# Recurrent part of a decoder: output product in three passes by block pairs, second norm on ScalarE, weight halves split at other places

## What is computed

```python
x = layernorm(x, ln0_w, ln0_b)
for l in range(4):
    h = layernorm(x, ln1_w[l], ln1_b[l])
    hh = time_shift(h)                       # the token before
    xk, xv, xr = (h * t[l] + hh * (1 - t[l]) for t in (tmk, tmv, tmr))
    k, v, sr = xk @ Wk[l].T, xv @ Wv[l].T, sigmoid(xr @ Wr[l].T)
    x = x + (sr * wkv(time_decay[l], time_first[l], k, v)) @ Wo[l].T
    h = layernorm(x, ln2_w[l], ln2_b[l])
    hh = time_shift(h)
    xk, xr = h * cmk[l] + hh * (1 - cmk[l]), h * cmr[l] + hh * (1 - cmr[l])
    kf = square(relu(xk @ Wck[l].T))         # 1024 hidden units
    x = x + sigmoid(xr @ Wcr[l].T) * (kf @ Wcv[l].T)
```

## Times and profile before

| what | us |
|---|---|
| median of 3 runs | 1903.39 (1900.92 to 1904.49) |
| profiled execution, its own time | 1903.27 |
| its span | 1901.6 |
| PE busy | 1777.8 (93%) |
| DVE busy | 1233.4 (65%) |
| ACT busy | 841.2 (44%) |
| mean granted clock of TensorE | 0.97 of 2.4 GHz |

### The profile page before, as it was taken

One profiled execution on the slowest core, in us unless ns is written; L12 is line 12 of the kernel. 1 busy time (PEld: TensorE's weight loads), 2 busy tenths in 40 slices (PEclk: granted clock), 3 DMA queues, 4 the chain that ended last, 5 costly groups with the idle time before them and its releaser, 6 DMA issues.

```text
span 1901.6 us, 26356 instructions
## 1 busy us (share of the span) xinstructions
PE 1777.8 (93%) x10124; PEld 1527.4 (80%) x10124; DVE 1233.4 (65%) x1953; ACT 841.2 (44%) x1304; POOL 3.6 (0%) x26
## 2 busy tenths in 40 slices
PE   2399999999999988889799999999999999999997
PEld 1277787877787767788789899889998898998896
DVE  6889999989999943788644445445445444454445
ACT  3465676665667634344332333333333323333333
POOL 0000000000000000000000000000000000000000
PEclk9699999999999998899899999999999999999999
DMA  3000001001001002111021111011100001011001
GB/s 111 5 23 17 10 25 40 6 8 43 17 12 50 1 0 88 52 43 37 10 77 34 34 34 34 0 33 33 33 33 0 33 33 33 33 34 38 1 1 39
DMA packets 35274, 56.54 MB, mean 30 GB/s; under 512 B 3094, under 2 KB 20476, under 8 KB 34684
## 3 DMA queue, kind: packets, MB, share of 16 engines
q1 hardware_dynamic: 35196, 55.47, 9.0%
HBM read 51.79 MB, written 3.67 MB: 29 GB/s over the span
## 4 chain that ended last, share of the span: by engine, by line
PE 49%; DVE 1%; ACT 0%; issue 0%; ACTq 0%; DVEq 0%
PE fbanks L1662 16%; PE fbank L1662 16%; PE fbank L1678 16%; DVE acc L1517 0%; DVE fst L1543 0%; PE fbank L52 0%; DVE xk L1541 0%; ACT acc L1633 0%; PE fbanks L1695 0%; ACT acc L1610 0%; DVE fmv L1546 0%; DVE fyy L1557 0%; DVE frstd L1558 0%; DVE fyy L1556 0%; ACTq L1340 0%
## 5 line engine op out<-in xcount | busy, mean ns | idle before, releaser
L1493 DVE TENSOR_TENSOR hf<-sil,fbanks 128x512 f32<-128x512 f32 (+1 forms) x128 | 79.4, 620 | 332.1 <-PE fbanks L1662 273.4
L1601 ACT ACTIVATE sil<-fbanks 128x512 f32<-128x512 f32 (+1 forms) x128 | 69.6, 544 | 442.2 <-PE fbanks L1662 442.2
L1678 PE MATMUL fbank<-wl,hh 128*128 128x256 f32 x896 | 250.3, 279 | 0.0
L1678 PE MATMUL fbank<-wh,hl 128*128 128x256 f32 x896 | 250.1, 279 | 0.0
L1678 PE MATMUL fbank<-wh,hh 128*128 128x256 f32 x896 | 250.1, 279 | 0.0
L1493 DVE TENSOR_TENSOR hf<-sil,fbank 128x512 f32<-128x512 f32 (+1 forms) x128 | 79.5, 621 | 149.8 <-PE fbank L1662 142.8
L715 PE MATMUL pair<-wcv,kf 128*112 128x256 f32 x768 | 176.1, 379 | 0.0
L1678 PEld LDWEIGHTS fbank<-wl,hh 128*128 128x128 f32 x896 | 168.3, 188 | 2.2
L1678 PEld LDWEIGHTS fbank<-wh,hh 128*128 128x128 f32 x896 | 168.4, 188 | 1.8
L1678 PEld LDWEIGHTS fbank<-wh,hl 128*128 128x128 f32 x896 | 168.4, 188 | 0.0
L1500 DVE TENSOR_TENSOR hl<-hf,hh 128x512 fp32r<-128x512 f32 (+1 forms) x256 | 158.3, 618 | 0.0
(11 more groups left out here) (237 smaller groups left out, 3478.3 us busy)
## 6 DMA issues: line engine op xcount, KB each, us to landing
raw<-in_w_gate SPq DMA_DIRECT2D x16, 512.0 KB, 3.8
raw<-in_w_up SPq DMA_DIRECT2D x16, 512.0 KB, 4.7
raw<-in_w_down SPq DMA_DIRECT2D x16, 512.0 KB, 5.6
raw<-in_w_ck SPq DMA_DIRECT2D x4, 1024.0 KB, 4.8
wcv<-in_w_cv SPq DMA_DIRECT2D x4, 768.0 KB, 4.4
raw<-in_ctx_t SPq DMA_DIRECT2D x4, 750.0 KB, 6.4
ct<-in_ctx_t SPq DMA_DIRECT2D x4, 750.0 KB, 5.0
x<-in_x SPq DMA_DIRECT2D x4, 448.0 KB, 6.2
```

Source lines behind the costliest of these rows:

```text
L1493: dve.tensor_tensor(hf[i][:, 0:w], sil[i][:, 0:w], bank[2 * i + 1][:, 0:w], ALU.mult).then_inc(hf_ready, 1)
L1601: act.activation(sil[f % 2][:, 0:w], bank[2 * (f % 2)][:, 0:w], ACT.Silu).then_inc(sil_ready, 1)
L1678: ins = pe.matmul(bank[4 + 2 * (t % 2) + i // 2][:, (i % 2) * C:(i % 2 + 1) * C], a[t % 2][:, f, i * P:(i + 1) * P], m[h][:, DOWN + f * C: ...
```

## The change

- The whole channel output is split in three matmuls. Weights wcvh and wcvl hold all eight blocks, plain wcv and its load are gone, the stage is loaded with all 1 MB of wcv. ACT writes a high part and DVE a low part of all four pairs of the hidden activation. `channel_out` runs over pairs of blocks outside and sequences inside, two pairs before the transposes of norm 1 and two behind them.
- Norm 2 is normalised by ACT, like norm 1, with a shift that DVE writes. ACT's normalise 1 goes ahead of the seed of norm 2.
- The mixes for cr and ck lose their difference: ACT writes h of the token before, scaled by 1 - mu (`past`), and DVE adds h times mu to it.
- DVE's numerator goes ahead of the mixes of norm 1, so ACT's copy of v can come sooner. `diff` shares memory with `dk`, `ckl` with `mix_ck`, `kfl` with `kf`.
- High and low parts of wck are taken just before `high_ck` and just after `low_ck`. The high part of wcv is taken right behind the gate, its low part behind the sums. `low_kf` 1 and 2 lie on either side of the sums, `low_kf` 3 in the next step behind the statistics of norm 2.

```diff
-SPLIT = 2
-NAMES = ["ln1w", "ln1b", "tmk", "tmv", "tmr", "td", "u", "ln2w", "ln2b", "cmk", "cmr", "w"]
+FT = F // P
+NAMES = ["ln1w", "ln1b", "tmk", "tmv", "tmr", "td", "u", "ln2w", "ln2b", "cmk", "cmr", "w", "pmk", "pmr"]
 PRM = {n: i for i, n in enumerate(NAMES)}
-NPRM = len(NAMES)
+NPRM, NPRM_IN = len(NAMES), NAMES.index("w")
...
-        wcvh, wcvl = sb("wcvh", [P, SPLIT * C], F32R), sb("wcvl", [P, SPLIT * C], F32R)
-        wcv = sb("wcv", [P, (F // P - SPLIT) * C])
...
-        ckh, ckl = sb("ckh", [P, CB, G * T], F32R), sb("ckl", [P, CB, G * T], F32R)
-        kf = [sb(f"kf{i}", [P, 2, G * T]) for i in range(4)]
-        kfh, kfl = sb("kfh", [P, SPLIT, G * T], F32R), sb("kfl", [P, SPLIT, G * T], F32R)
+        ckh = sb("ckh", [P, CB, G * T], F32R)
+        with nc.sbuf_tensor("mix_ck", [P, CB, G, T], FP32) as t:
+            mixed["ck"] = t
+        ckl = sb("ckl", [P, CB, G * T], F32R)
+        with nc.sbuf_tensor("kf", [P, FT, G * T], FP32) as t:
+            kf = [t[:, 2 * j:2 * j + 2] for j in range(FT // 2)]
+        t = sb("kfl", [P, FT, G * T], F32R)
+        kfl = [t[:, 2 * j:2 * j + 2] for j in range(FT // 2)]
+        kfh = sb("kfh", [P, FT, G * T], F32R)
...
-                if name == "cv":
-                    w = w[:, 0:SPLIT * C]
...
+            def mix2(m, i, name, mu):
+                for b in range(CB):
+                    dve.wait_ge(past_ready, 2 * CB * m + CB * i + b + 1)
+                    dve.scalar_tensor_tensor(mixed[name][:, b], h[2][:, b, :, 1:T1], param(m, b, mu),
+                                             mixed[name][:, b], ALU.mult, ALU.add).then_inc(mix2_ready, 1)
...
             first_norm(0)
             for s in range(-3, STEPS + 1):
                 if valid(s):
                     after(add_wkv(s))
                     stats(2, chunk(s))
-                    if s % GROUPS == 0:
-                        l = s // GROUPS
-                        low_weights(2 * l, wckl, wckh, ck_done, 4 * GROUPS * l)
+                if valid(s - 1):
+                    low_kf(s - 1, 3)
                 if valid(s + 1):
                     wkv_denominator(s + 1)
                 if valid(s):
                     rsqrt(2, s)
-                    normalise(2, xn[2], chunk(s), xn_ready[2])
+                    set_shift(2)
+                if valid(s + 1):
+                    wkv_numerator(s + 1)
                 if valid(s + 2):
-                    n = difference(1, s + 2)
-                    mix(1, s + 2, ("k", "v", "r"), ("tmk", "tmv", "tmr"), mix1_ready, n)
+                    mix1(s + 2)
                 if valid(s):
-                    n = difference(2, s)
-                    mix(2, s, ("cr",), ("cmr",), mix2_ready, n)
+                    mix2(s, 0, "cr", "cmr")
                 if valid(s - 1):
                     gate_channel(s - 1)
                 if valid(s):
-                    mix(2, s, ("ck",), ("cmk",), mix2_ready, n)
-                if valid(s + 1):
-                    wkv_numerator(s + 1)
+                    mix2(s, 1, "ck", "cmk")
                 if valid(s - 1):
                     add_channel(s - 1)
                 if valid(s):
                     low_ck(s)
+                    if s % GROUPS == 0:
+                        l = s // GROUPS
+                        low_weights(2 * l, wckl, wckh, ck_done, 4 * GROUPS * l)
                 if valid(s + 3):
                     if s + 3 >= GROUPS:
...
                     wkv_out(s + 1)
                 if valid(s + 2):
                     wkv_arguments(s + 2)
-                if valid(s) and s % GROUPS == 0:
-                    l = s // GROUPS
-                    low_weights(2 * l + 1, wcvl, wcvh, cv_done, 2 * GROUPS * l)
                 if valid(s):
                     low_kf(s, 0)
                 if valid(s + 3):
                     rsqrt(1, s + 3)
-                    set_shift(s + 3)
+                    set_shift(1)
                 if valid(s):
-                    for j in range(1, SPLIT // 2):
-                        low_kf(s, j)
+                    low_kf(s, 1)
                 if valid(s + 2):
                     wkv_sums(s + 2)
+                if valid(s):
+                    if s % GROUPS == 0:
+                        l = s // GROUPS
+                        low_weights(2 * l + 1, wcvl, wcvh, cv_done, 2 * GROUPS * l)
+                    low_kf(s, 2)
...
+            def past(m, i, name, mu):
+                act.wait_ge(h_ready[2], CB * (m + 1))
+                if m:
+                    act.wait_ge(*((cr_done, m) if name == "cr" else (ck_done, 4 * m)))
+                for b in range(CB):
+                    act.activation(mixed[name][:, b], h[2][:, b, :, 0:T], ACT.Copy, scale=param(m, b, mu))\
+                        .then_inc(past_ready, 1)
+            def normalise(k, m):
+                act.wait_ge(shift_ready[k], m + 1)
                 xc = x[:, (m % GROUPS) * G:(m % GROUPS + 1) * G, :]
                 for i in range(G):
-                    ins = act.activation(xn[1][:, i, :], xc[:, i, :], ACT.Identity, bias=shift[:, i:i + 1],
-                                         scale=rstd[1][:, i:i + 1])
-                ins.then_inc(xn_ready[1], 1)
+                    ins = act.activation(xn[k][:, i, :], xc[:, i, :], ACT.Identity, bias=shift[k][:, i:i + 1],
+                                         scale=rstd[k][:, i:i + 1])
+                ins.then_inc(xn_ready[k], 1)
...
             def hidden(m, j):
                 act.wait_ge(ck_done, 4 * m + j + 1)
-                split = 2 * j < SPLIT
-                if m and split:
-                    act.wait_ge(kfl_ready, SPLIT // 2 * (m - 1) + j + 1)
-                if m and not split:
+                if m and j == 0:
                     act.wait_ge(cv_done, 2 * m)
                 t = kf[j]
-                act.activation(t[:], pair[HIDDEN[j]][:, :, 0:G * T], ACT.Relu).then_inc(relu_done, 1)
+                act.activation(t, pair[HIDDEN[j]][:, :, 0:G * T], ACT.Relu).then_inc(relu_done, 1)
                 act.wait_ge(relu_done, 4 * m + j + 1)
-                act.activation(t[:], t[:], ACT.Square).then_inc(square_done, 1)
-                if not split:
-                    return
+                act.activation(t, t, ACT.Square).then_inc(square_done, 1)
                 act.wait_ge(square_done, 4 * m + j + 1)
-                if m and j == 0:
-                    act.wait_ge(cv_done, 2 * m)
-                act.activation(kfh[:, 2 * j:2 * j + 2], t[:], ACT.Copy).then_inc(kfh_ready, 1)
+                act.activation(kfh[:, 2 * j:2 * j + 2], t, ACT.Copy).then_inc(kfh_ready, 1)
...
             rsqrt0(0, 0)
             for s in range(-3, STEPS + 1):
-                if valid(s) and s % GROUPS == 0:
-                    l = s // GROUPS
-                    high_weights(2 * l, wckh, ck_done, 4 * GROUPS * l)
                 if valid(s + 1):
                     wkv_exp(s + 1, 2)
+                if valid(s + 2):
+                    normalise(1, s + 2)
                 if valid(s):
                     rsqrt0(2, s)
-                if valid(s + 2):
-                    normalise1(s + 2)
                 if valid(s + 1):
                     reciprocal0(s + 1)
                 if valid(s + 2):
                     norm_out(1, s + 2, pair[2], "ln1w", "ln1b")
                 if valid(s):
+                    normalise(2, s)
                     norm_out(2, s, pair[0], "ln2w", "ln2b")
+                    past(s, 0, "cr", "pmr")
                 if s < 0:
                     rsqrt0(1, s + 3)
                 if valid(s + 2):
                     out(s + 2, 0, kp[:, :, :, 1:T1], k_out)
                 if valid(s):
+                    past(s, 1, "ck", "pmk")
+                    if s % GROUPS == 0:
+                        l = s // GROUPS
+                        high_weights(2 * l, wckh, ck_done, 4 * GROUPS * l)
                     high_ck(s)
                 if valid(s + 2):
                     if s + 2:
...
                     out(s + 2, 2, th[:], th_ready, ACT.Tanh, 0.5)
                 if valid(s):
                     gate(s)
+                    if s % GROUPS == 0:
+                        l = s // GROUPS
+                        high_weights(2 * l + 1, wcvh, cv_done, 2 * GROUPS * l)
                 if valid(s + 2) or valid(s):
                     act.preload_act_table_set(LN_EXP)
                 if s >= 0 and valid(s + 3):
...
                 if valid(s + 2):
                     wkv_exp(s + 2, 0)
                     wkv_exp(s + 2, 1)
-                if valid(s) and s % GROUPS == 0:
-                    l = s // GROUPS
-                    high_weights(2 * l + 1, wcvh, cv_done, 2 * GROUPS * l)
...
+            def channel_out(m, pairs):
+                for p in pairs:
+                    pe.wait_ge(kfl_ready, FT // 2 * m + p + 1)
+                    for i in range(G):
+                        for f in range(2):
+                            j = 2 * p + f
```

(74 more changed lines are left out.)

41 lines of the change are left out of this document (13 added, 28 removed).

## The result

| | before | after |
|---|---|---|
| median us | 1903.94 (1900.92 to 1905.38, 4 runs) | 1927.9 (1926.12 to 1928.33, 4 runs) |
| profiled execution's span | 1901.6 | 1926.6 |
| PE, DVE, ACT busy us | 1777.8, 1233.4, 841.2 | 1760.9, 1252.2, 960.7 |

The ratio is 1.0126, with a 95% interval of 1.0109 to 1.0144: slower by 24 us. The forecast was 1922, its range 1897 to 1936.

What follows compares the result with a forecast made beforehand. PE bound the recurrent part, DVE close; after the change ACT's string would. From 1903.27 us: head to second K +4.9, layer 0's ordinary steps -1.9, later first steps +25.5, other ordinary steps -3.6, tail -6, giving 1922; range 1897 to 1936.

Steps and rivals of the forecast that it cites:

- ordinary step: Recurrent steps not first in a layer: from one k product start (K) to the next 39.95 us, before 40.55.
- ACT's wait for the load: First step of a layer: ACT idles some 2.5 us behind the gate until the load of wcv lands at K + 16.1.
- channel output of the first step from: First step of a layer: PE idles 7.5 us for the low part of wcv, ready at K + 34.5.
- loss to the clock, a first step: First step of a layer: PE's idle lowers the granted clock, costing 2.4 us, bounds 0 to 3.4.
- first step: First step of each layer, K to K: 49.9 us against 41.4, so +8.5.
- head, up to the K of step 0: Start up to step 0's k product: numerator slips into a wait, low wck leaves the path; 4.5 us less.
- tail: Steps 14, 15 and the end: channel output is on the path three times, each 1.9 us or more shorter; 6 less.
- attention and experts: Code behind the recurrent part: untouched by the change, so no change in time.
- Rival A: Recurrent part: PE's saving decides, all 16 steps fall to 38.6 us and the first-step wait is filled; 1872 us; chance 0.07.
- Rival C: Ordinary step: three full engines, new forms at upper bounds or handshakes adding up, 41 instead of 39.95; 1935 us; chance 0.12.
- Rival B: First step: if wcv is loaded before the gate ends, ACT never stands; step near 43, 1895 us; chance 0.11.
- Rival D: First step: only the wait is lost, not the clock, four times 2.4 less; 1912.5 us; 0.68 together with the main case.

Runs made afterwards that it cites:

- e5: Changed kernel plus 56 idle matmuls on PE ahead of the wait for the low part of wcv: 1919.5 us, against 1927.9 for the changed kernel.
- e6: Changed kernel plus two extra ACT copies into an unused tile in steps 0 to 13, ahead of the exponentials: 1946.6 us, ordinary step 40.95.
- e7: Changed kernel plus the same two extra ACT copies, but ahead of the first table load: 1927.7 us, ordinary step 39.88.
- e9: Changed kernel with ACT's eu and normalise 1 ahead of hidden 2 and 3, and DVE's low kf 2 behind the denominator: 1930.9 us.
- e11: Changed kernel with norm 2 normalised on DVE again, all else kept: 1935.9 us, ordinary steps 40.8.
- e10: e3 plus a new order on ACT (normalise 1, affine part, normalise 2 earlier) and DVE (numerator behind norm 1's mixes): 1873.6 us, ratio 0.9840 to the kernel before.
- e1: Changed kernel with a staging tile of its own for wcv, its load issued a layer early: 1918.2 us, ratio 1.0067 to the kernel before.
- e2: Changed kernel with the low part of wcv taken on DVE ahead of the sums, one stage: 1914.7 us, ratio 1.0046 to the kernel before.
- e3: Changed kernel with both own stage for wcv and low part of wcv ahead of the sums: 1900.8 us, ratio 0.9982 to the kernel before.
- e8: Changed kernel with ACT's eu and normalise 1 ahead of hidden 2 and 3, and DVE's low kf 3 behind rsqrt 2: 1940.5 us.

## Why the prediction was right, point by point

| step of the prediction | forecast | measured |
|---|---|---|
| PE's channel output | 11.5 us, 0.118 a matmul | 5.7 for each half, 0.118 |
| ordinary step | 39.95 | 39.87 |
| PE's wait ahead of the transposes | 1.3 | 1.20 |
| ACT's wait for the load | 2.5, high wcv from K + 16.1 | 2.32, K + 16.0 |
| channel output of the first step from | K + 34.5, idle 7.5 | K + 34.7, idle 7.51 |
| loss to the clock, a first step | 2.4 (0 to 3.4) | mean 2.2 by e5 (1.3 to 2.8) |
| first step | 49.9 | 48.8, 49.9, 50.5 |
| head, up to the K of step 0 | -4.5 | -1.7 |
| tail | -6 | -6.1 |
| attention and experts | 0 | +4.3 |

**The ordinary step.** PE's saving was real, 1.9 us, and 0.7 of it arrived. e6 and e7 show why: ACT's string from the gate to normalise 1 sets the step. e9 and e11 show the second path, DVE's to mix_k, right behind it. Rival A falls with that. It is what e10 comes near to, but only with another order on two engines. Rival C did not come: the new forms cost what their nearest rows did, the scaled pair 1.22 or 1.23 against 1.21.

**The first step.** Both waits are where they were put, and e1, e2 and e3 give their price: 10 and 13 us alone, 27 together. Rival B named the right mechanism. Its condition, a load that is done before the gate ends, is what e1 makes, and e3 lands where B's arithmetic pointed (first step near 43, 1895 forecast, 1900.8 measured). What B left out is that the wait for the low part has to go as well. The rule of the Trainium skill that ACT and DVE are strictly first in, first out (TensorE: Matmul & The Clock Gate, "Engine queue depths") agrees again: nothing on ACT passed high wcv in its 2.32 us.

**The clock.** I took 2.4 us from one idle of 4.29 in the tail. e5 puts it at 2.2 in the mean and at 1.3 to 2.8 in single steps, inside my bounds. Rival D, that the clock costs nothing, is refuted.

**What was off.** The head: the numerator did slip into the wait for h, but of the 3.3 us it freed most was lost at once. The exponentials stand behind ACT's tanh of r, which waits for PE, and DVE stood 2.74 us for them, where before it did not wait at all. I had walked DVE through the head, but not ACT. The last link is another too: DVE's difference ahead of mix_k comes 2.6 us earlier than before (94.77 against 97.38), but K only 1.7, right behind the transposes of norm 2, for which PE stood 7.48 us until ACT's normalise 2. DVE and PE of after:

```profile
75.89 2.04 DVE L348 TENSOR_TENSOR_SCAN bb<-e1b,e2b 128x904 f32<-128x904 f32 x1 [2.74 <-ACT e2b L575]
...
96.07 1.76 PE L670 MATMUL pair<-ident,xn 112*128 112x112 f32 x8 [7.48 <-ACT xn L533]
```

The seven traces in which the head has the order of after (after, e1, e2, e3, e5, e6, e7) put the K of step 0 at 96.7 to 99.2 us, so the -1.7 of one execution is uncertain by more than 1 us, but none reaches the -4.5.

And attention: I had put the code that is not touched at nothing. Two such stretches, before and after, cut at matching places; behind the length, columns are busy us and count of PE, PEld, DVE, ACT and POOL, then the clock, the DMA share and GB/s:

```profile
900.00:960.00 60.00, 48.76 (x301) 45.35 (x301) 37.98 (x58) 21.71 (x34) 0.10 (x1) 0.77 0.18 56
```

```profile
921.00:984.00 63.00, 51.96 (x298) 47.99 (x298) 37.93 (x59) 22.30 (x34) 0.10 (x1) 0.72 0.19 61
```

The same work took 3 us longer at a lower mean clock (0.72 against 0.77). It is not chance in this one execution. In all twelve traces with the changed recurrent part, whatever it took, the time from the first product of attention to the end is 1156.2 to 1159.7 us; in the one trace of the kernel before it is 1152.5. A stretch of 48 us that starts 183 us behind that product has a clock of 0.81 in before and of 0.69 to 0.73 in the twelve, here before, after and e10:

```profile
932.00:980.00 48.00, 43.51 (x218) 37.91 (x219) 29.62 (x47) 22.25 (x35) 0.10 (x1) 0.81 0.24 76
...
952.70:1000.70 48.00, 43.71 (x200) 38.11 (x199) 26.50 (x44) 20.53 (x31) 0.10 (x1) 0.72 0.23 76
...
897.60:945.60 48.00, 43.71 (x200) 38.09 (x199) 26.63 (x44) 20.59 (x31) 0.10 (x1) 0.72 0.22 76
```

Why the clock is lower there stays open. It is also open whether every execution of the kernel before is as fast there as its one trace, since its runs lie between 1900.9 and 1907.9. The head (+2.8) and attention (+4.3), less some 1 us in the other terms, are the difference between 1922 and 1928; that the total fell inside the range although these two terms were put wrong owes something to the width of the range.

## What to carry to other kernels

Busy shares do not tell what an engine can still take: the same two copies cost 1.08 us a step at one place of ACT's order and nothing at another. Before adding work to an engine in strict order, add up the string from the event that starts it to the event that the bound engine waits for, and do the same for the engine behind it; and for each wait in it, a load above all, name all that is queued behind. When a change is a loss, look whether its work or its order costs: here 1.3% slower became 1.6% faster with every matmul, copy and subtraction of the change kept, and one staging tile more.

## What the runs showed that I had not expected

- The price of an idle of PE by the clock is not a constant. The idle was 7.51 us in all four first steps of after, and behind it the clock cost 2.5, 1.3, 2.4 and 2.8 us against e5. Nor does it belong to the step: in e7, where the first steps have the same order and the same idle of 7.51, the channel output until K took 15.6 us in step 4, where after took 14.1, and 14.4 in step 8, where after took 15.2.
- An ordinary step of PE took 38.43 to 38.47 us in e10 with no wait in it, where the pieces of the earlier trace rows with the new channel output add up to 38.65.
- Two repairs that each win 10 and 13 us won 27 together, and one that took 5.6 us out of the longest string (e8) lost 12.6. In the first case one wait stood behind the other; in the second the new order put a wait of 1.65 us into DVE's path to mix_k.
